# One core, eight sequences: own orders for the first and last turn, the loop written out, the LoRA in two token halves, layernorm a turn earlier

## The chip, the core and the metric

The kernel runs on one core of a Trainium2 chip. The metric is the device time of one launch in microseconds. A launch handles 8 sequences of 512 tokens with 128 features.

## What is computed

Each sequence is layer-normalised; the result goes through a selective state-space block with complex states and through a three-layer MLP with weights of plus or minus one, and both are added to the input:

```python
xn = _layernorm(x, axis=-1)
x = x + _L0_attn_ref(xn, ...) + _L0_ffn_ref(xn, ...)
# attention part: projections z, x, B, C, dt; a causal convolution of 4 taps with silu on x, B, C
lora  = jnp.tanh(x @ theta_w1) @ theta_w2            # 128 -> 48 -> 128
theta = jnp.clip(theta_base + lora, -pi/2, pi/2)
log_z = complex(-(lambda_base + eta * theta**2) * dt, theta * dt)
S_t   = exp(log_z_t) * S_(t-1) + B_t * (x_t * dt_t);  y_t = Re(C_t S_t) + x_t * D
g = y * silu(z);  out = (g * rsqrt(mean(g*g) + eps) * norm_w) @ out_proj_w.T
# MLP: 128 (as x, -x) -> 512 -> 512 -> 128 with relu * 2
```

## The kernel before, in words

**Stages and turns.** One sequence n passes through two stages. Its front makes the convolved projections, the phases and decays, and the MLP; its back, one turn later, makes the attention products G, y, the gated result and the output. Turn n does the front of n and the back of n-1, and at its end the first projections of n+1. So turn 0 has no back, turn 7 is the last with a front and has no next sequence, and turn 8 has only a back. Turns 1 to 6 are a hardware loop (`Fori`) of three passes with two turns each, on all five engines. A second, more general pass over all sequences stands behind an `If` and is not entered for these inputs.

**Order.** Every engine executes a list in an order written by hand (`pipelined` of each block); semaphores with counted steps tie the lists together. An instruction that waits holds up all that stand behind it on its engine.

**TensorE (PE).** `lora1` (L1281) multiplies with 48 columns of `TW1`. Then come, for the back, `g_products` (L1360, tiles of 32 rows), which wait for `add_mlp` of the turn before (`s_mo`), and `g_across` (L1370), which waits for GpSimd's Bre and Bim (`s_bk`). `z_products` (L1312), `lora2` (L1317), `dt_spread` (L1323), the transposes of Bre and Bim (L1381), and y (L1392, L1399, L1408, L1428) follow. Then `mlp0` for tiles 0 and 1 (L1331), `out_products` (L1451), the transposes of the next xn (L1264), `mlp0` for tiles 2 and 3, the sums of squares (L1443), `mlp1` (L1341, L1342) in two pairs of tiles with x projections of the next sequence (L1295) behind each, `mlp_out` (L1350), which waits for the last low half of h1, and the B and C projection (L1305).

**VectorE (DVE).** After `add_mlp` (L746): four convolution taps (L555, L558), `layernorm` of n+1 (L501 to L507), the four masked copies of G (L677), theta (L564), phases (L571 to L590), the states, the gating (L734), cumulated decays (L604, L605), the low halves of h0 (L742), products with the decay in PSUM (`decayed`, L648), `final`, xd = x times dt (L546), the steps of dt, the low halves of h1 (L742), `decayed` of U, which waits for GpSimd's U, and `largest` (L670), directly ahead of `add_mlp`.

**ScalarE (ACT).** silu of x, tanh, silu of B and C, silu of z (L992), theta's input `tin` (L996), copies, xn, sine and cosine (L1007 to L1010), relus and exponentials.

**GpSimd (POOL).** rstd of n+1, then `c_rotated` (six operations on 128x512, from the end of L1010), `rms_of` (L1143, waits for the mean squares), `b_times_rotated` (six, L1162 to L1165, giving Ure and Uim) and `b_and_k` (six, L1190 to L1193, giving Bre and Bim). Each triple is two products and their sum or difference.

**SyncE (SP)** loads x two sequences ahead into two buffers, repeats the rows of B and C through DMAs after `silu_bc`, and stores the output.

## Time and profile before

| | us |
|---|---|
| median of 3 timed runs | 372.28 (367.29 to 373.07) |
| the profiled execution, own time | 364.21 |
| its span, first to last instruction | 361.6 |
| PE busy | 301.3 (83%) |
| DVE busy | 270.0 (75%) |
| POOL busy | 199.6 (55%) |
| ACT busy | 173.9 (48%) |

The span is what the rows below add up to; the execution's own time is 2.6 us more. Shares of busy time are means over the whole span. Matmuls overlap each other, so the time between the starts of two groups says more than the length of one.

### The profile page before, as it was taken

Reading aid. Unit: us, or ns where it says so; the run is one execution under the profiler, and the core shown is the slowest. Engines: PE = TensorE matmul, PEld = TensorE weight load, DVE = VectorE, ACT = ScalarE, POOL = GpSimd, SP = SyncE. Lnnn points to the kernel's source line nnn. Section 1 sums busy time; section 2 is a strip of 40 time slices with the busy share of each in tenths; the row PEclk is TensorE's granted clock in tenths of the full one; section 3 lists DMA queues with packets and bytes.
Section 4 is the critical chain, followed back from the end, with each engine's and each line's share of the span. In section 5 each row is a group of like instructions: output and inputs, shape, how many; then the busy total and the mean of one; then the engine's idle time right before and its main releaser. Section 6 shows DMA issues by size and latency. Waiting matters only on the chain.

```text
span 361.6 us, 9844 instructions
## 1 busy us (share of the span) xinstructions
PE 301.3 (83%) x3887; PEld 211.1 (58%) x3887; DVE 270.0 (75%) x661; ACT 173.9 (48%) x305; POOL 199.6 (55%) x172
## 2 busy tenths in 40 slices
PE   0477079998999898999999997989998999884780
PEld 0353035776577655675667665766676667643670
DVE  2698767698869896798789885789698968973321
ACT  0306752477446834486438732683467446651010
POOL 0000399318881789138952896078926891499201
PEclk9999759999999999999999998999999999998996
DMA  6200400131113110320113011311032101300001
GB/s 179 53 1 4 106 9 0 34 83 38 29 32 77 44 32 8 77 67 2 29 54 96 2 29 33 92 29 29 3 82 66 31 2 46 75 8 24 2 2 34
DMA packets 19095, 14.81 MB, mean 41 GB/s; under 512 B 5045, under 2 KB 14826, under 8 KB 19050
## 3 DMA queue, kind: packets, MB, share of 16 engines
q1 hardware_dynamic: 16090, 13.67, 14.6%
q10 hardware_dynamic: 2960, 0.49, 0.8%
q8 instruction: 34, 0.56, 0.6%
q14 instruction: 11, 0.09, 0.1%
HBM read 3.67 MB, written 2.10 MB: 16 GB/s over the span
## 4 chain that ended last, share of the span: by engine, by line
PE 50%; DVE 34%; issue 6%; ACT 3%; POOL 3%; DMA 2%; SPq 1%; DVEq 0%; POOLq 0%
PE bank L1295 11%; PE bank L1341 7%; PE bank L1342 7%; PE bank L1350 4%; PE bank L1428 3%; PE bank L1443 3%; DVE GT L677 3%; DVE bcsum L558 3%; DVE phl L572 3%; DVE cum L604 3%; PE bank L1360 2%; DVE gT L734 2%; DVE h0l L742 2%; DVE cum L605 2%; PE bank L1293 2%
## 5 line engine op out<-in xcount | busy, mean ns | idle before, releaser
L1341 PE MATMUL bank<-h0h,W 128*128 128x512 f16 x128 | 50.0, 390 | 2.2 <-DVE h0l L742 1.4
L1342 PE MATMUL bank<-h0l,W 128*128 128x512 f16 x128 | 49.8, 389 | 0.0
L1162 POOL TENSOR_TENSOR btmp<-cres,Xre 128x512 f32<-128x512 f32 x8 | 10.2, 1272 | 71.0 <-ACT Xre L1010 71.0
L1295 PE MATMUL bank<-XW,xh 128*128 128x256 f16 x256 | 48.7, 278 | 0.0
L1137 POOL TENSOR_TENSOR rstd<-vare,minus_half 128x4 f32<-128x4 f32 x8 | 8.4, 1049 | 53.2 <-DVE negmean L507 53.2
L1295 PE MATMUL bank<-XW,xl 128*128 128x256 f16 x128 | 35.5, 277 | 0.0
L1042 ACT ACTIVATE h1h<-bank 128x512 f16<-128x512 f32 x32 | 19.0, 593 | 32.2 <-PE bank L1342 31.3
L1295 PEld LDWEIGHTS bank<-XW,xh 128*128 128x128 f16 x256 | 25.4, 99 | 6.8 <-issue 0.2
L742 DVE SCALAR_TENSOR_TENSOR h0l<-bank,h0h 128x512 f16<-128x512 f32 x32 | 22.1, 689 | 8.1 <-ACT h0h L1042 7.8
L742 DVE SCALAR_TENSOR_TENSOR h1l<-bank,h1h 128x512 f16<-128x512 f32 x32 | 22.0, 686 | 7.2 <-ACT h1h L1042 7.0
L677 DVE TENSOR_TENSOR GT<-bank,const 128x512 f32<-128x512 f32 x32 | 19.8, 681 | 8.9 <-PE bank L1370 8.9
L1341 PEld LDWEIGHTS bank<-h0h,W 128*128 128x128 f16 x128 | 13.4, 105 | 17.9 <-issue 2.9
L1042 ACT ACTIVATE h0h<-bank 128x512 f16<-128x512 f32 x32 | 18.1, 591 | 7.1 <-PE bank L1332 7.1
L1143 POOL TENSOR_TENSOR rms<-msq,minus_half 128x4 f32<-128x4 f32 x8 | 8.2, 1019 | 23.3 <-DVE msq L738 23.3
L1342 PEld LDWEIGHTS bank<-h0l,W 128*128 128x128 f16 x128 | 12.8, 100 | 14.1 <-issue 1.4
L1392 PE MATMUL bank<-GT,xd 128*64 128x128 f32 x256 | 20.3, 279 | 0.4 <-issue 0.4
L1350 PE MATMUL bank<-W,h1h 128*128 128x128 f16 x128 | 16.4, 228 | 4.8 <-DVE h1l L742 4.8
L746 DVE SCALAR_TENSOR_TENSOR o<-bank,sffn,xtok 128x512 f32<-128x512 f32 x8 | 6.0, 750 | 18.9 <-PE bank L1350 18.9
L1451 PE MATMUL bank<-OW,gT 128*128 128x128 f32 x128 | 16.4, 281 | 4.5 <-DVE gT L734 4.5
L1451 PEld LDWEIGHTS bank<-OW,gT 128*128 128x128 f32 x128 | 14.9, 191 | 8.2 <-DVE gT L734 8.2
L1399 PE MATMUL bank<-skip_eye,x 128*64 128x128 f32 x256 | 19.5, 273 | 0.0
L558 DVE SCALAR_TENSOR_TENSOR bcsum<-bank,cw,bcsum 128x511 f32<-128x511 f32 (+2 forms) x24 | 18.0, 749 | 0.8
(201 smaller groups left out, 916.7 us busy)
## 6 DMA issues: line engine op xcount, KB each, us to landing
xtok<-in_x SPq DMA_DIRECT2D x8, 256.0 KB, 2.7
cres<-bc SPq DMA_DIRECT2D x32, 64.0 KB, 2.1
cims<-bc SPq DMA_DIRECT2D x32, 64.0 KB, 2.1
bres<-bc SPq DMA_DIRECT2D x32, 64.0 KB, 2.4
bims<-bc SPq DMA_DIRECT2D x32, 64.0 KB, 2.1
out<-osb SPq DMA_DIRECT2D x8, 256.0 KB, 2.3
const<-constants SPq DMA_DIRECT2D x1, 576.0 KB, 5.6
KT<-in_in_proj_w SPq DMA_DIRECT2D x1, 320.0 KB
```

Of the source, the lines that this page charges most:

```text
L558: step(V.scalar_tensor_tensor(bcsum[:, late:], bank[2][:, 0:T - late], cw[:, 2, k:k + 1], bcsum[:, late:], ALU.mult, ALU.add), linked=k > 0)
L572: step(V.tensor_tensor_scan(phl[:], c_("restart"), ph[:], 0.0, ALU.mult, ALU.add), linked=False)
L677: V.tensor_tensor(GT[:, h, :, :], gbanks[fast][h][:].rearrange("p (c t) -> p c t", t=CH), view(const, 0, 128, mask, [[0, NCH], [1, CH]]), ...
L742: V.scalar_tensor_tensor(lo[:, f, :], bank[4 + f % 2][:], 0.0, high[:, f, :], ALU.max, ALU.subtract).then_inc(sig.sem, 1)
L1042: step(sig, A.activation(hi[:, f, :], bank[4 + f % 2][:], ACT.Relu))
L1295: last = M.matmul(dst, tok(x, c, k), w[:, k, :], start=False, stop=(k == TAPS - 1 and q == 2))
L1341: M.matmul(bank[4 + f % 2][:], w, h0h[:, k, :], start=(k == 0), stop=False)
L1342: last = M.matmul(bank[4 + f % 2][:], w, h0l[:, k, :], start=False, stop=(k == MT - 1))
L1350: last = M.matmul(bank[4][:, D * c:D * c + D], h[:, k, CH * c:CH * c + CH], W2[:, k, :], start=(k == 0 and r == 0), stop=(k == MT - 1 and ...
L1392: last = M.matmul(y_part(h, CH * c, CH), xd[:, c, HEAD * h:HEAD * h + HEAD], GT[:, h, c, :], start=(c == 0), stop=True, skip_group_check=True)
L1399: last = M.matmul(y_part(h, CH * c, CH), x2s[p][:, c, HEAD * h:HEAD * h + HEAD], skip_eye[:, h, :], start=False, stop=True, skip_group_che ...
L1451: last = M.matmul(out_in[:, D * c:D * c + D], gT[:, h, CH * c:CH * c + CH], OW[:, h, :], start=(h == 0), stop=(h == 1))
```

## The change

- The loop of turns 1 to 6 is written out on all five engines; the waits have constants in place of registers.
- x has three buffers. SP loads three sequences ahead, and `layernorm(n + 2)` stands right ahead of `add_mlp(n)`; in turn n it no longer stands between taps and G.
- The LoRA works on halves of 256 tokens. `lora1` is six matmuls on two column tiles of 64; tanh works on 128x256; `lora2` is two matmuls on row tiles 0 and 64, the second into bank 1, and stands behind `dt_spread` and behind the wait for two emptied G banks. `tin` is two activations. `theta_w2` is loaded twice, and two memsets fill TW1.
- The gating is four operations of 256 columns in place of two of 512; `out_products` waits for each half of the tokens. The sums of squares stand between `mlp0` tiles 2 and 3, and the first tile of `mlp1` waits for the low halves of h0 one by one.
- The third transposed chunk of Bre, Bim goes to bank 5 and waits for all of G.
- Turn 0 has an order of its own on PE, DVE and ACT, with no other stage between the MLP layers' tiles. In turns 0 and 7 VectorE makes Uim and Bim, in turn 0 also Rim, by three operations each (`other_half`), and GpSimd makes only the real parts. In turn 7 xd stands behind `add_mlp`.

The diff, cut to its core and moved left by 8 columns (in order SP, DVE, ACT, POOL, PE):

```diff
-    (tw2[:], a["theta_w2"]),
+    (tw2[0:LORA, :], a["theta_w2"]),
+    (tw2[HALF:HALF + LORA, :], a["theta_w2"]),
...
+        load(1, 1, 1, None)
+        load(2, 2, 2, None)
         repeat_bc(0, True)
-        with sp.Fori(0, SEQS // 2 - 1) as i:
+        for i in range(SEQS // 2 - 1):
             for p in range(2):
-                load(2 * i + p + 2, 2 * i + p + 2, p)
+                n = 2 * i + p
+                if n + XBUFS < SEQS:
+                    load(n + XBUFS, n + XBUFS, n % XBUFS, n)
                 repeat_bc(2 * i + p + 1, True)
                 store(2 * i + p, 2 * i + p, p)
...
+        step(V.tensor_tensor(shape(tmpa), *first, ALU.mult), linked=False)
+        step(V.tensor_tensor(shape(tmpb), *second, ALU.mult))
+        step(V.tensor_tensor(dst[:], tmpa[:], tmpb[:], op))
+    def whole(t):
+        return t[:]
+    def subs(t):
+        return t[:].rearrange("p (c t) -> p c t", t=SUB)
+    def rotated_im(n):
+        v.wait_ge(c_in.sem, c_in.done(n))
+        v.wait_ge(a_trig.sem, a_trig.done(n))
+        other_half(chain(s_rim, 0), Rim, (cres[:], psn), (cims[:], pcs), ALU.add, whole)
+    def b_times_rotated_im(n):
+        v.wait_ge(b_in.sem, b_in.done(n))
+        v.wait_ge(s_rot.sem, s_rot.done(n))
+        other_half(chain(s_im, EDGES.index(n)), Uim, (bres[:], Rim[:]), (bims[:], Rre[:]), ALU.add, whole)
+    def b_and_k_im(n):
+        step = chain(s_im, EDGES.index(n))
+        step.count[0] = 3
+        br, bi = (view(x, 0, 128, SUB - 1, [[SUB, NSUB], [0, SUB]]) for x in (bres, bims))
+        step.link()
+        v.wait_ge(s_kq.sem, s_kq.at(n, 2))
+        other_half(step, Bim, (subs(Kim), br), (subs(Kre), bi), ALU.subtract, subs)
...
-    def gated(n, p, half):
+    def gated(n, p):
         step = chain(s_gate, n)
-        step.count[0] = half
-        v.wait_ge(t_y.sem, t_y.at(n, half + 1))
-        step(V.tensor_tensor(gT[:, half, :], bank[6 + half][:], z2s[p][:, half, :], ALU.mult), linked=False)
+        v.wait_ge(t_y.sem, t_y.done(n))
+        for lo in (0, T // 2):
+            cols = slice(lo, lo + T // 2)
+            for half in range(2):
+                step(V.tensor_tensor(gT[:, half, cols], bank[6 + half][:, cols], z2s[p][:, half, cols], ALU.mult),
+                     linked=False)
...
         def gates(slot):
             if has_back:
...
                 h0_low(n, 0)
         if has_front:
             bc_taps(n)
-        if next_loaded is not None:
-            layernorm(n + 1, 1 - p, next_loaded)
         if has_back:
             for h in EMPTIED:
                 g_base(n - 1, True, h)
...
             h0_low(n, 2)
+            decayed(n, 0, (0,))
             h0_low(n, 3)
-            decayed(n, 0)
-        if next_loaded is not None:
+            decayed(n, 0, (1,))
+        if has_next:
             xn_low(n + 1)
         if has_back:
             mean_squares(n - 1)
         if has_front:
             decayed(n, 1)
             h1_low(n, 0)
+        if has_front and not has_next:
+            b_times_rotated_im(n)
+            h1_low(n, 1)
+            final(n - 1, pq, stored)
+            h1_low(n, 2)
+            decayed(n, 2)
+            h1_low(n, 3)
+            b_and_k_im(n)
+            largest(n)
+            add_mlp(n, n % XBUFS)
+            x_times_dt(n, p)
+            return
         if has_back:
             final(n - 1, pq, stored)
         if has_front:
             h1_low(n, 1)
-        if next_loaded is not None:
+        if has_next:
             dt_input(n + 1)
         if has_front:
             x_times_dt(n, p)
-        if next_loaded is not None:
+        if has_next:
             dt_steps(n + 1)
         if has_front:
             h1_low(n, 2)
             decayed(n, 2)
             h1_low(n, 3)
             largest(n)
-            add_mlp(n, p)
+            early_layernorm(n + 2)
+            add_mlp(n, n % XBUFS)
+    def first_turn(n, p):
+        bc_taps(n)
+        early_layernorm(n + 1)
+        thetas(n)
+        def lows(slot):
+            if slot < 2:
+                h0_low(n, 2 * slot)
+                h0_low(n, 2 * slot + 1)
+        phases(n, lows)
+        exponents(n, True)
+        rotated_im(n)
+        decayed(n, 0)
+        xn_low(n + 1)
+        decayed(n, 1)
+        h1_low(n, 0)
+        b_times_rotated_im(n)
+        h1_low(n, 1)
+        dt_input(n + 1)
+        x_times_dt(n, p)
+        dt_steps(n + 1)
+        h1_low(n, 2)
+        h1_low(n, 3)
+        decayed(n, 2)
+        b_and_k_im(n)
+        largest(n)
+        early_layernorm(n + 2)
+        add_mlp(n, n % XBUFS)
...
-        pipelined(2 * i + 1, 1, 0, 16 * i + 1, True, True, 16 * i + 32)
-        pipelined(2 * i + 2, 0, 1, 16 * i + 1, True, True, 16 * i + 32)
+    first_turn(0, 0)
+    for i in range(SEQS // 2 - 1):
+        pipelined(2 * i + 1, 1, 0, 16 * i + 1, True, True, True)
...
-        step(a_th, A.activation(tin[:], bank[3][:], ACT.Identity, bias=base[:, 0:1]))
+        for lo, of in ((0, bank[3]), (T // 2, bank[1])):
+            cols = slice(lo, lo + T // 2)
+            step(a_th, A.activation(tin[:, cols], of[:, cols], ACT.Identity, bias=base[:, 0:1]))
...
+            step(a_kt, A.copy(KT[:, 2, :, :], bank[5][:, 0:256]))
         else:
             step(a_kt, A.copy(KT[:, 2:4, :, :], bank[1][:]))
...
+    def first_turn(n, p):
+        silu_x(n, p, 0)
+        silu_x(n, p, 1)
+        tanh_lora(n)
+        dt_repeated(n)
+        silu_bc(n, True)
+        theta_input(n)
+        mlp_high(a_h0, t_h0, h0h, n, (0, 1))
+        silu_z(n, p)
+        mlp_high(a_h0, t_h0, h0h, n, (2, 3))
+        decay_rate(n)
+        normalised(n + 1, (n + 1) % XBUFS)
+        trig(n)
+        decays(n, True, 0)
+        xn_t(n + 1)
+        decays(n, True, 1)
+        mlp_high(a_h1, t_h1, h1h, n, (0, 1))
+        dt_exp(n + 1)
+        mlp_high(a_h1, t_h1, h1h, n, (2, 3))
...
-    def turned(sig, n, re, im, left):
+    def turned(sig, n, re, im, left, other=None):
         (a, b), (c, d) = left
-        for k, (dst, f1, f2, op) in enumerate(((re, c, d, ALU.subtract), (im, d, c, ALU.add))):
+        for k, (dst, f1, f2, op) in enumerate(((re, c, d, ALU.subtract), (im, d, c, ALU.add))[:1 if other else 2]):
             P.tensor_tensor(btmp[0][:], a[:], f1, ALU.mult).then_inc(sig.sem, 1)
             P.tensor_tensor(btmp[1][:], b[:], f2, ALU.mult).then_inc(sig.sem, 1)
             g.wait_ge(sig.sem, sig.at(n, 3 * k + 2))
-            P.tensor_tensor(dst[:], btmp[0][:], btmp[1][:], op).then_inc(sig.sem, 1)
-            g.wait_ge(sig.sem, sig.at(n, 3 * k + 3))
-    def c_rotated(n):
+            if other:
+                g.wait_ge(*other)
...
         if has_next:
             rstds(n + 1)
-        if has_front:
-            c_rotated(n)
+        shared = has_front and not (has_back and has_next)
+        if has_front:
+            c_rotated(n, (s_rim.sem, s_rim.done(0)) if shared and not has_back else None)
         if has_back:
             rms_of(n - 1)
         if has_front:
-            b_times_rotated(n)
-            b_and_k(n, s_kq, 0)
-            b_and_k(n, s_kq, 1)
+            b_times_rotated(n, (s_im.sem, s_im.at(EDGES.index(n), 3)) if shared else None)
+            b_and_k(n, s_kq, 0, (s_im.sem, s_im.done(EDGES.index(n))) if shared else None)
+            if not shared:
+                b_and_k(n, s_kq, 1)
     rstds(0)
     pipelined(0, False, True, True)
-    with g.Fori(0, SEQS // 2 - 1) as i:
+    for i in range(SEQS // 2 - 1):
         pipelined(2 * i + 1, True, True, True)
...
-            last = M.matmul(bank[3][0:LORA, :], w[:], x[:, PAD:], start=(k == 0), stop=(k == 2))
+            for part in range(2):
+                last = M.matmul(bank[3][HALF * part:HALF * part + HALF, 0:T // 2], w[:],
+                                x[:, PAD + T // 2 * part:PAD + T // 2 * part + T // 2],
+                                start=(k == 0), stop=(k == 2), skip_group_check=True)
         last.then_inc(t_l1.sem, 1)
     def x_part(n, half, part):
...
+            rows = slice(HALF * part, HALF * part + LORA)
+            last = M.matmul(into, tw2[rows, :], th1[rows, :], start=True, stop=True)
+        last.then_inc(t_l2.sem, 1)
     def dt_spread(n):
         pe.wait_ge(s_conv.sem, s_conv.done(n))
...
             if f >= 2:
                 pe.wait_ge(s_h1l.sem, s_h1l.at(n, f - 1))
             for k in range(MT):
+                if f == 0:
+                    pe.wait_ge(s_h0l.sem, s_h0l.at(n, max(k, 2) + 1))
                 w = W1[:, k, 128 * f:128 * f + 128]
...
-    def k_transposes(n, chunks):
-        for c in range(chunks):
-            for r, k in enumerate((Bre, Bim)):
-                q = 2 * c + r
-                last = M.transpose(bank[q // 4][:, 128 * (q % 4):128 * (q % 4) + 128], k[:, CH * c:CH * c + CH], ident)
-            if c in (1, chunks - 1):
-                last.then_inc(t_kt.sem, 1)
+    def k_transposes(chunks, into):
+        for q, (c, k) in enumerate((c, k) for c in chunks for k in (Bre, Bim)):
+            last = M.transpose(into[:, 128 * q:128 * q + 128], k[:, CH * c:CH * c + CH], ident)
+        last.then_inc(t_kt.sem, 1)
...
-        pe.wait_ge(s_gate.sem, s_gate.done(n))
         for c in range(NCH):
+            if c % 2 == 0:
+                pe.wait_ge(s_gate.sem, s_gate.at(n, c + 2))
             for h in range(2):
                 last = M.matmul(out_in[:, D * c:D * c + D], gT[:, h, CH * c:CH * c + CH], OW[:, h, :],
...
-            lora2(n)
             dt_spread(n)
         if has_back:
             pe.wait_ge(s_g[True].sem, s_g[True].at(b, 2))
-            k_transposes(b, NST[True])
+        if has_front:
+            lora2(n)
+        if has_back:
+            k_transposes((0, 1), bank[0])
             y_wait(b, True, n if has_front else b)
+            k_transposes((2,), bank[5])
             within(b, 0)
             skipped(1 - p, 0)
             within(b, 1)
...
             last.then_inc(t_y.sem, 2)
+        if has_front and not has_back:
+            mlp0(n, range(MT))
+            mlp1(n, (0, 1))
+            xn_transposed(n + 1)
+            dt_products(n + 1)
+            x_products(n + 1, 1)
+            mlp1(n, (2, 3))
+            x_products(n + 1, 0)
+            mlp_out(n)
+            bc_products(n + 1)
+            return
         if has_front:
             mlp0(n, (0, 1))
         if has_back:
...
         if has_front:
-            mlp0(n, (2, 3))
+            mlp0(n, (2,))
         if has_back:
             sums_of_squares(b)
+        if has_front:
+            mlp0(n, (3,))
         if has_front:
             mlp1(n, (0, 1))
             if has_next:
```

## Rows read from the trace of the kernel before

**Rows 1.** Stretches of the span: length, busy time and count per engine, granted clock, DMA.

```profile
66.05:103.30 37.25, 36.03 (x488) 25.50 (x485) 31.92 (x75) 21.58 (x38) 21.25 (x19) 1.00 0.17 44
140.54:180.12 39.58, 36.32 (x488) 25.68 (x485) 31.94 (x75) 21.47 (x38) 24.90 (x22) 1.00 0.16 42
217.36:258.30 40.94, 37.67 (x489) 26.52 (x485) 31.94 (x75) 21.48 (x38) 24.89 (x22) 0.96 0.16 40
```

**Rows 2.** The chain that ended last, at the loop's first jump back: start, us, what.

```profile
142.97 2.04 issue
```

**Rows 3.** Timeline of PE in turn 2: start, us, line, tiles, count, idle time before.

```profile
105.66 0.40 PE L1281 MATMUL bank<-xh,TW 128*48 128x512 f16 x1
...
106.42 0.50 PE L1360 MATMUL bank<-Ure,Kre 32*128 32x128 f32 x8
106.75 0.40 PE L1360 MATMUL bank<-Uim,Kim 32*128 32x128 f32 x8
...
110.92 1.12 PE L1317 MATMUL bank<-th,tw 48*128 48x512 f32 x2
111.97 0.66 PE L1323 MATMUL bank<-const,dtb 128*128 128x128 f32 x4
...
140.38 0.22 PE L1350 MATMUL bank<-W,h1h 128*128 128x128 f16 x1
```

**Rows 4.** Timeline of DVE in turn 2.

```profile
105.12 0.75 DVE L746 SCALAR_TENSOR_TENSOR o<-bank,sffn,xtok 128x512 f32<-128x512 f32 x1 [2.06 <-PE bank L1350]
...
108.86 0.86 DVE L501 BATCH_NORM_STATS2 st<-xtok 128x6 f32<-128x128 f32 x4
...
110.25 0.16 DVE L507 TENSOR_SCALAR negmean<-mv 128x4 f32<-128x4 f32 x1
...
112.80 0.43 DVE L564 TENSOR_SCALAR theta<-tin 128x512 f32<-128x512 f32 x1
```

**Rows 5.** Timelines of ACT and of POOL in turn 2.

```profile
112.08 0.69 ACT L996 ACTIVATE tin<-bank,base 128x512 f32<-128x512 f32 x1
...
118.82 0.70 ACT L1010 ACTIVATE Xre<-pabs,halfpi 128x512 f32<-128x512 f32 x1
...
128.50 1.02 POOL L1143 TENSOR_TENSOR rms<-msq,minus_half 128x4 f32<-128x4 f32 x1 [1.06 <-DVE msq L738]
...
136.85 1.27 POOL L1165 TENSOR_TENSOR Uim<-btmp 128x512 f32<-128x512 f32 x1
...
143.85 1.27 POOL L1193 TENSOR_TENSOR Bim<-btmp 128x512 f32<-128x512 f32 x1
```

**Rows 6.** Timelines of DVE and POOL where both read SBUF.

```profile
139.96 0.33 DVE L670 TENSOR_TENSOR most<-most,beyond 128x1 f32<-128x1 f32 x1
...
139.21 1.06 POOL L1191 TENSOR_TENSOR btmp<-Kim,bims 128x512 f32<-128x512 f32 x1
...
57.44 1.26 DVE L546 TENSOR_TENSOR xd<-x,dt 128x1024 f32<-128x1024 f32 x1
...
57.70 2.13 POOL L1165 TENSOR_TENSOR Uim<-btmp 128x512 f32<-128x512 f32 x1
```

**Rows 7.** Timelines of PE and DVE in turn 0 and at its end.

```profile
45.65 1.08 PE L1264 MATMUL bank<-const,xn 128*128 128x128 f32 x4 [9.97 <-DVE cum L604]
...
69.18 0.50 PE L1360 MATMUL bank<-Ure,Kre 32*128 32x128 f32 x8
...
67.87 0.75 DVE L746 SCALAR_TENSOR_TENSOR o<-bank,sffn,xtok 128x512 f32<-128x512 f32 x1 [3.40 <-PE bank L1350]
```

**Rows 8.** Timelines of PE and DVE in turns 7 and 8.

```profile
331.78 0.29 PE L1350 MATMUL bank<-W,h1h 128*128 128x128 f16 x1 [4.80 <-DVE h1l L742]
...
335.85 0.50 PE L1360 MATMUL bank<-Ure,Kre 32*128 32x128 f32 x8 [0.84 <-DVE o L746]
...
349.25 2.05 PE L1451 MATMUL bank<-OW,gT 128*128 128x128 f32 x16 [1.41 <-DVE gT L734]
...
329.84 0.69 DVE L648 TENSOR_TENSOR Ure<-Ure,bank 128x512 f32<-128x512 f32 x1 [3.12 <-POOL Uim L1165]
```

More of the change, by code:

```diff
@@ L839, in _ @@
             pair(CB[0:1, :], CB[BLK:BLK + 1, :], cb_row[:], BIAS_SCALE)
-            pair(TW1[0][:], TW1[1][:], tw1[:])
+            for k in range(2):
+                setup(V.memset(TW1[k][:, LORA:], 0.0), False)
+            pair(TW1[0][:, 0:LORA], TW1[1][:, 0:LORA], tw1[:])
             v.wait_ge(set_pe, 1)
@@ L1523, in _ @@
             pipelined(0, 0, False, True, True)
[L1524 removed]
+            for i in range(SEQS // 2 - 1):
                 pipelined(2 * i + 1, 1, True, True, True)
```

114 lines of the change are left out of this document (61 added, 53 removed).

## The prediction

> **What bounds the kernel now.** I cut the span at the start of `mlp_out` in each turn and read busy times per stretch. A turn takes 37.25 us, of which PE is busy 36.03 [rows 1]; four of the six turns that end inside the loop are like that. The turns that cross the loop's jump back take 39.58 and 40.94 us [rows 1]. Next I read the chain of waits: at the first jump it holds PE for 2.04 us with no releaser [rows 2], at the second likewise, and after the second the granted clock of the stretch is 0.96. Last I read the timelines of one normal turn, engine by engine [rows 3 to 5], because a PE with 1.2 us idle looks like the bound and may not be.
>
> It is not alone. A second loop runs through GpSimd and has four pieces. (a) From the start of `g_products` at 106.42 [rows 3] through z, `tin` (ends 112.77), theta at 112.80 and the phases to the end of the cosine at 119.52 is 13.1 us [rows 4, 5]. (b) GpSimd's rotations, rms and U, to the end of Uim at 138.12, are 18.6, with 1.06 of waiting for the mean squares [rows 5]. (c) The two decayed products and the last low half, to `mlp_out` at 140.38 [rows 3], are 2.26; the same three operations with nothing else in the way take 1.94 in turn 7 (329.84 to 331.78) [rows 8], so 0.3 is slack. (d) `mlp_out` to the next `g_products` is the rest of the period, 3.28. The sum is 37.24.
>
> **The loop written out.** The excess over 37.24 is 2.34 and 3.70, together **6.0 us**. Passing from one turn to the next inside a pass has no such row. I take all 6.0. The ends are 4.1 (only the two holds of 2.04, if the slow clock behind them returns from another idle stretch) and 6.5, if constants in place of registers also take something from each turn.
>
> **A normal turn, six times.** *Layernorm*: 1.55 us on DVE (108.86 to 110.41) leaves the place ahead of G [rows 4]. It doesn't shorten the path by that: theta at 112.80 follows directly on `tin`, which ends at 112.77 [rows 4, 5]. So what counts is when `tin` comes. At its new place it falls into the 2.06 us for which DVE waits for `mlp_out` [rows 4], 0.5 of which is left. *LoRA*: `lora1` spans 0.76 to the next group, `lora2` 1.05 [rows 3]. Operations on different row tiles overlap in the trace already: eight matmuls of 128 columns on tiles of 32 rows stand in one row of 0.40 us [rows 3]. Halved, they take about 0.43 and 0.53. `lora1` gives 0.33 to (d). `lora2` ends no earlier, since `dt_spread` (0.49) now goes first: 0.49 + 0.53 is today's 1.05. Two activations in place of one of 0.69 are an estimated 0.8, so `tin` is 0.1 late. Between the last matmul of `lora1` (about 106.33) and `g_products` there is 0.1, which I take as the price of a change of tile shape. The Trainium skill (TensorEngine Tiling (Array Packing), Key Properties) says that changing the tiling mode drains the engine; the change adds two such changes a turn, and by that page the six turns would give 1.2 us less, which the trace neither shows nor excludes. *Gates, sums, mlp0 and mlp1*: the new order fills most of PE's 1.2 us of idle time [rows 1], but only the mean squares, some 0.15 earlier, lie on GpSimd's loop. Where PE gets ahead, it waits at `mlp_out` for the last low half, so (c) is 1.95. *Bim* ends 7.0 us after Uim (143.85 + 1.27 against 138.12) [rows 5]; `g_across`, 2.0 behind the start of `g_products`, would come at 1.95 + 2.95 + 2.0 = 6.9 and waits 0.1.
>
> New turn: (a) 13.2, (b) 18.45, (c) 1.95, (d) 2.95, 0.1 for Bim: 36.65 to 36.7. That is **0.55 a turn, 3.3 us** in six. Upper end: PE alone, 36.03 minus 0.8 of LoRA plus some waits, 36.0 a turn, 7 us. Lower end: the layernorm's small operations are held up by GpSimd, below, nothing or slightly less.
>
> **How DVE and GpSimd share SBUF.** xd, two inputs in SBUF, ran from 57.44 to 58.70; GpSimd's operation that started at 57.70 took 2.13 us, where its kind takes 1.27 [rows 5, 6]: it stood for 0.86. The other way round, `largest` on 128x1 started at 139.96 and ended at 140.29, as GpSimd's ended at 140.27 [rows 6]. So such operations exclude each other. That decides what sharing with DVE is worth. Each triple moved to DVE in turns 0 and 7 takes 3.9 us from GpSimd but puts about 2 us of DVE into which GpSimd cannot work: about 2 gained where GpSimd is the path, not 3.9. The Trainium skill (SBUF — State Buffer, Who interferes with whom) speaks of an exclusive lock on a shared port pair, and says that a Vector operation with at most one SBUF input outside the two-port modes doesn't contend. By that rule the moved layernorm's statistics pass freely and only its small scalar operations can be held.
>
> **Turn 7.** `mlp_out` waits 4.80 us at 331.78 for GpSimd's Uim, DVE having waited 3.12 [rows 8]. New: Uim's three operations on DVE start behind the first low half of h1 and end near 325.5, GpSimd's Ure at 326.9. The second low half and `final` then delay the others; the last low half ends near 329.7. So `mlp_out` starts 2.1 earlier, and about 0.9 more goes behind it: from there to `g_products` at 335.85 are 4.07 us, against 3.28 in a normal turn, though B, C and `lora1` are not among them; with 1.9 us of idling before it in place of 4.8, `mlp_out` should run nearer to its normal pace. **3.0 us** plus 0.15 from (b); ends 1.5 and 4. Bim on DVE starts only then and covers itself with `mlp_out`; xd (1.26) behind `add_mlp` is covered by `g_products`.
>
> **Turn 0.** PE idles 9.97 us before 45.65, in the middle of the first sequence's MLP [rows 7]. In the new order the MLP's first tiles fill that gap, and `mlp_out` comes about 2 earlier, at 63.8. But DVE then still has two products, three operations of Bim, `largest` and a layernorm of 1.55, together about 5.1 behind the last low half at 62.7, ahead of `add_mlp`: 67.8, where it starts at 67.87 today [rows 7]. `g_products`, today at 69.18, follows at 68.55: **0.6 us**. The cosine comes 2.4 later than today, since ACT has four h0 tiles, silu of z and the rate first; Rim on DVE gives that back. Ends: 2 lost, 3 gained. More setup (two memsets, a DMA on the ACT queue, one of 256 KB on SP's) lies beside PE's and DVE's longer chain to the first projections: nothing, at most 1 lost.
>
> **Turn 8.** The first half of the outputs waits for 0.7 of gating in place of 1.2, so `out_products`, held 1.41 at 349.25 [rows 8], starts 0.6 earlier, and the end with it. The third transposes behind all of G cost 0.2. **0.4 us**; ends 0 and 1.
>
> **Sum.** 6.0 + 3.3 + 3.1 + 0.6 + 0.4 = 13.4. The profiled execution took 364.21, so its like would take 350.8. The median of the runs is 372.28, 8.1 above that execution. Taking off 13.4 gives 358.9; since part of the spread between runs may come from the jumps and the slow clock behind them, I take 1.9 more: **357 us**.
>
> **Rivals.** *(1) The moved layernorm holds the turn.* In its new place GpSimd is always busy with B and K, and the scalar operations and the memset may each be held for up to one GpSimd operation of 1.06 to 1.27 [rows 5, 6]. Only 0.5 of the 2.06 is spare, and PE needs `add_mlp` about 0.5 later than it needs `mlp_out`'s end. One hold is free, two cost 0.6 a turn, the whole gain. Then the turns stay at 37.2 and the time is 360. No row has a layernorm beside a busy GpSimd. Chance 0.28. *(2) PE is the bound*, (b) being slack that other orders take up: 36.0 a turn, 7 us in place of 3.3, and the time is 353. For it: PE busy 36.03 of 37.25. Against it: the four pieces close exactly. 0.15. *(3) The jumps' cost stays.* The 2 us come back at another point of the code, and the gain is 7.4: 365. Against it: turn 0 into 1 and the middle of each pass show no stall. 0.05. *(4) Slower.* Straight code has to be fetched throughout, and PE stalls as at the jumps, 2.04 us [rows 2], in every turn: seven stalls and the clock behind some, about 19 us in place of 6. With 7.4 gained elsewhere it ends 6 above today, 378. It decides from one stall a turn on. Against it: the two turns of a pass are straight code and run without one. 0.04. *The change doesn't do what it says*: tiles of the LoRA that do not overlap make `tin` 0.5 late, six times, and the time 360 as in (1). 0.06.
>
> **Chances.** My forecast 0.42, (1) with its twin 0.34, (2) 0.15, (3) 0.05, (4) 0.04. The range 348 to 364.5 takes in the first three with the ends of turns 0 and 7. What a measurement here can tell from no change is 2%, 7.4 us, so faster means below 364.8: 0.88; within 0.08; slower 0.04.
>
> **What would show it.** All turns alike, no "issue" row of 2 us between them; a period near 36.7 with `mlp_out` waiting for a low half that follows Uim at once (if it starts without a wait, PE is the bound); `add_mlp` starting at `mlp_out`'s end (later: rival 1); theta right behind `tin`; GpSimd operations of 2 us beside DVE's triples; turn 7 near 34. Wrong would be a stall in straight code, or a turn 0 longer than today's.

## The result and the profile after

| | before | after |
|---|---|---|
| median of 4 timed runs, us | 369.78 (366.02 to 373.07) | 354.38 (353.19 to 356.84) |
| the profiled execution, own time | 364.21 | 354.44 |
| its span | 361.6 | 352.6 |

The ratio is 0.9654, with a 95% interval of 0.9615 to 0.9694: faster, by 3.5%. Each ratio leaves out slow runs, those over 1.5% above the fastest of their kernel (here those of the kernel before above 372 us), so it says about 13 us, where the medians of all runs differ by 15.4. The forecast was 357, in a range of 348 to 364.5. The two spans differ by 9.0 us, though, where the sum said 13.4.

The windows of the changed kernel, cut at the start of `g_products` (columns: window and length, busy time of PE, PEld, DVE, ACT, POOL with instructions, PEclk, DMA share, GB/s):

```profile
69.75:106.94 37.19, 35.57 (x490) 25.55 (x490) 32.20 (x78) 20.66 (x38) 22.38 (x20) 1.00 0.17 44
218.74:256.01 37.27, 35.64 (x491) 25.54 (x489) 32.06 (x78) 21.33 (x39) 24.89 (x22) 1.00 0.17 44
293.30:327.25 33.95, 27.69 (x415) 19.33 (x413) 29.83 (x55) 16.64 (x30) 17.18 (x15) 1.00 0.16 41
327.25:352.60 25.35, 14.15 (x327) 12.63 (x327) 8.11 (x20) 2.11 (x4) 1.51 (x2) 0.87 0.05 14
```

Against [rows 1]: no turn is longer than the others, so what the jumps cost is gone, but a normal turn (a turn from 1 to 6 that no jump and no slow clock lengthens) is still 37.27 where it was 37.25. Over turns 1 to 6 it is 223.55 us for 229.49, 5.9 gained, all of it by the loop. Turn 7 gained 3.2 (33.95 for 37.18), turn 8 0.4, and turn 0 lost 0.6 (`g_products` at 69.75 for 69.18 in [rows 7]). The sum is 9.0.

Why not the normal turn? GpSimd and VectorE of the changed kernel, from their timelines of one turn (start, length, engine, line, what; in brackets the idle time before it and who ended it):

```profile
238.83 1.27 POOL L1277 TENSOR_TENSOR Rim<-btmp 128x512 f32<-128x512 f32 x1
241.43 1.02 POOL L1253 TENSOR_TENSOR rms<-msq,minus_half 128x4 f32<-128x4 f32 x1 [1.34 <-DVE msq L780]
```

```profile
239.33 0.69 DVE L784 SCALAR_TENSOR_TENSOR h0l<-bank,h0h 128x512 f16<-128x512 f32 x1 [0.47 <-ACT h0h L1132]
239.94 0.68 DVE L657 TENSOR_TENSOR Kim<-Xim,bank 128x512 f32<-128x512 f32 x1
240.53 0.69 DVE L521 SCALAR_TENSOR_TENSOR xl<-bank,xh 128x512 f16<-128x512 f32 x1
241.14 0.15 DVE L780 TENSOR_SCALAR msq<-bank 128x4 f32<-128x4 f32 x1
...
253.14 0.86 DVE L510 BATCH_NORM_STATS2 st<-xtok 128x6 f32<-128x128 f32 x4
...
255.02 0.75 DVE L788 SCALAR_TENSOR_TENSOR o<-bank,sffn,xtok 128x512 f32<-128x512 f32 x1 [0.33 <-PE bank L1473]
```

GpSimd's rms waits 1.34 us for the mean squares, where it waited 1.06 [rows 5]. PE starts the sums of squares 1.2 us earlier behind the cosine's end, but VectorE gets to `msq` only behind the low half of tile 3, Kim and xl, and tile 3 now comes later, since the sums stand ahead of it on PE. The same view shows that rival 1 didn't happen: the layernorm ends before `mlp_out` does. The other loss is ahead of theta: z starts 4.70 us after `g_products` for 4.60, `tin` takes 0.84 in two operations for 0.69, and theta waits for it:

```profile
225.39 0.43 DVE L573 TENSOR_SCALAR theta<-tin 128x512 f32<-128x512 f32 x1 [0.81 <-ACT tin L1086]
```

### The profile page after: what moved, and what is told of

It reads as the page before. It is cut to its first block, busy times and chain, and to the rows that moved or that the text cites. A ratio compares the mean times of both kernels' runs of the same rounds, so it can differ in the third digit from the quotient of the medians.

```text
span 352.6 us, 9459 instructions
## 1 busy us (share of the span) xinstructions
PE 297.9 (84%) x3927; PEld 209.6 (59%) x3927; DVE 282.9 (80%) x694; ACT 172.3 (49%) x313; POOL 181.6 (52%) x157
## 4 chain that ended last, share of the span: by engine, by line
DVE 34%; PE 32%; POOL 16%; ACT 8%; issue 6%; DMA 2%; SPq 1%; POOLq 0%; DVEq 0%
POOL btmp L1272 6%; PE bank L1483 5%; POOL btmp L1273 4%; PE bank L1549 4%; PE bank L1564 3%; PE bank L1473 3%; DVE gT L775 3%; PE bank L1431 3%; DVE phl L581 3%; PE bank L1493 3%; DVE cum L613 2%; POOL Ure L1277 2%; POOL Uim L1277 2%; ACT z L1080 2%; POOL rms L1253 2%
## 5 line engine op out<-in xcount | busy, mean ns | idle before, releaser
L1414 PE MATMUL bank<-XW,xh 128*128 128x256 f16 x256 | 51.6, 289 | 0.0
L1414 PE MATMUL bank<-XW,xl 128*128 128x256 f16 x128 | 36.8, 288 | 0.0
L1414 PEld LDWEIGHTS bank<-XW,xh 128*128 128x128 f16 x256 | 26.3, 103 | 8.0 <-issue 0.9
L1132 ACT ACTIVATE h1h<-bank 128x512 f16<-128x512 f32 x32 | 18.1, 589 | 24.9 <-PE bank L1465 24.9
L1473 PE MATMUL bank<-W,h1h 128*128 128x128 f16 x128 | 15.2, 220 | 3.7 <-DVE h1l L784 3.7
L1564 PEld LDWEIGHTS bank<-const,gsq 128*128 128x128 f32 x128 | 15.5, 192 | 1.0
```

Source lines behind the costliest of these rows:

```text
L1132: step(sig, A.activation(hi[:, f, :], bank[4 + f % 2][:], ACT.Relu))
L1414: last = M.matmul(dst, tok(x, c, k), w[:, k, :], start=False, stop=(k == TAPS - 1 and q == 2))
L1473: last = M.matmul(bank[4][:, D * c:D * c + D], h[:, k, CH * c:CH * c + CH], W2[:, k, :], start=(k == 0 and r == 0), stop=(k == MT - 1 and ...
L1564: last = M.matmul(sums_in[:, c:c + 1], gsq[:, half, CH * c:CH * c + CH], all_ones(1), start=(half == 0), stop=(half == 1))
```

## The experiments

Every ratio is to the kernel before, run on the same chip. Within one kernel the timed runs spread over 0.7 to 7 us, so a period (`g_products` to `g_products`, in the profiled execution) tells more than a median here. A part of the spread has a cause that the profiles showed: **in some turns the granted clock falls for 3 to 4 us.**

### The jumps

```diff
-with pe.Fori(0, SEQS // 2 - 1) as i:
+for i in range(SEQS // 2 - 1):
```

The same on SP, DVE, ACT and POOL of the kernel before.

> The kernel before with nothing changed but the loop over turns 1 to 6, which is written out on every engine. Theory A (the jumps cost what the rows show): the turns that followed a jump lose their excess over 37.25 us, 2.3 and 3.7 us, so the profiled execution comes 6.0 us under the 361.6 us span of the kernel before, at 355.6, with every turn at 37.2, and the changed kernel's six equal turns of 37.27 us say that all else in a normal turn came to nothing. The median of the timed runs then falls by at least 6 us; the median of the kernel before lies 5.6 us over its profiled execution, and if that distance is jumps that cost more in other executions, the timed gain is 10 to 12 us and the spread of the timed runs shrinks to under 3 us. Rival B (the jump only shows a delay that something else would cause in these turns anyway): the turns of 39.6 and 40.9 us stay, and the gain is under 2 us.

Median 361.08 (360.29 to 366.65), ratio 0.9836 [0.9764, 0.9907], the span 357.4. Its turns, and two of the kernel before that [rows 1] doesn't hold:

```profile
106.88:144.19 37.31, 36.03 (x486) 25.48 (x485) 31.97 (x76) 21.61 (x38) 24.92 (x22) 1.00 0.17 44
144.19:182.71 38.52, 36.61 (x485) 25.66 (x485) 31.96 (x76) 21.66 (x38) 24.89 (x22) 1.00 0.17 43
182.71:220.02 37.31, 36.03 (x485) 25.49 (x485) 31.97 (x76) 21.61 (x38) 24.90 (x22) 1.00 0.18 44
```

```profile
106.42:145.78 39.36, 36.10 (x486) 25.51 (x485) 33.91 (x79) 21.58 (x38) 26.29 (x23) 1.00 0.19 49
183.24:223.25 40.01, 36.74 (x486) 25.59 (x485) 34.55 (x81) 21.58 (x38) 26.25 (x23) 0.98 0.18 48
223.25:261.42 38.17, 36.95 (x485) 26.42 (x484) 29.29 (x71) 21.48 (x38) 23.53 (x20) 0.97 0.15 36
```

Theory A holds, rival B falls: a turn that had a jump falls from 39.36 to 37.31. The 6.0 of the forecast are thus made up otherwise: two jumps of 2.1, and some 1.6 of slow clock (0.98 and 0.97, PE 0.7 and 0.9 busier) that the first jump didn't have and that straight code shows as well, below. The two jumps by themselves are worth 4.2. The Trainium skill (Runtime: NRT & Kernel Launch, Instruction fetch mechanics) says that a taken branch whose target isn't in the part of the code that is held must wait until it has been fetched; 2.1 us at each jump fit that, but no row here shows a fetch. One turn of e1 is 1.2 longer at full clock, with 0.37 of it a stall without a releaser; its cause stays open. The expected text was off in two numbers: the span came to 357.4 and not 355.6, since of its turns 1 to 6 that one was longer and turn 0 took 0.4 more, and the median fell by 5.2 and not by 6 or more.

### The mean squares

e2 moves them ahead of the low half of tile 3; e3 undoes PE's side of the edit.

```diff
 decayed(n, 0, (0,))
+mean_squares(n - 1)
 h0_low(n, 3)
 decayed(n, 0, (1,))
 xn_low(n + 1)
-mean_squares(n - 1)
```

> The changed kernel with one move on VectorE: mean_squares of the pair before stands ahead of h0_low of tile 3 instead of behind it, Kim and xl. Theory A (the normal turn gained nothing because the sum over mean squares, queued behind a tile that itself came later, holds GpSimd's rms by 1.34 us): the wait of rms falls to under 0.3 us, the stretch from the cosine's end to Uim's end from 18.93 to about 17.7, and the six periods from 37.27 to 36.0 to 36.4; the time falls by 5.5 to 8 us (six or seven turns of 0.9 to 1.27), to 346 to 349. Rival B (TensorE's order bounds the turn: busy 35.64 of 37.27 with the small waits that remain): periods stay above 37.0 and the time within 1.5 us of the changed kernel. Rival C: h0_low of tile 3 and what stands behind it, now later by the sum, holds TensorE's mlp1 and with it mlp_out: the period lengthens by up to 0.5 us, 3 us in all.

Median 355.67 (354.55 to 356.01), ratio 0.9698 [0.9644, 0.9751]; five of the six periods are 37.54 to 37.57, against 37.27. The wait of rms is gone (it follows Rim at once) and nothing is gained. Rival C in its effect, but by another mechanism. PE of e2, then VectorE ahead of that:

```profile
257.04 0.50 PE L1484 MATMUL bank<-Ure,Kre 32*128 32x128 f32 x8 [0.82 <-DVE o L788]
```

```profile
252.41 0.69 DVE L784 SCALAR_TENSOR_TENSOR h1l<-bank,h1h 128x512 f16<-128x512 f32 x1
253.01 1.08 DVE L708 TENSOR_TENSOR most<-most,beyond 128x1 f32<-128x1 f32 x1
254.02 0.86 DVE L510 BATCH_NORM_STATS2 st<-xtok 128x6 f32<-128x128 f32 x4
...
255.33 0.93 DVE L515 TENSOR_SCALAR vare<-mv 128x4 f32<-128x4 f32 x1
256.18 0.16 DVE L516 TENSOR_SCALAR negmean<-mv 128x4 f32<-128x4 f32 x1
256.25 0.74 DVE L788 SCALAR_TENSOR_TENSOR o<-bank,sffn,xtok 128x512 f32<-128x512 f32 x1
```

Two tiny operations, of 128x1 and 128x4, take 1.08 and 0.93 us, each until GpSimd's operation ends. In the changed kernel they took 0.33 and 0.17. That is rival 1, and it appears here, where GpSimd's row is early. The last of the six turns has no layernorm there, and its period is 36.66.

```diff
-mlp0(n, (2,))
+mlp0(n, (2, 3))
 sums_of_squares(b)
-mlp0(n, (3,))
```

> The changed kernel with TensorE's tile 3 of the first MLP product back ahead of the sums of squares (that one edit undone, VectorE's order as changed). Theory A (the edit turned round what it should do: the squares' sums came earlier by one tile, but the tile that VectorE handles ahead of the mean square came later): tile 3 ends some 1.7 us earlier, the sums some 0.5 later, the mean square comes 0.3 to 0.5 us earlier in the turn, and the period is 36.8 to 37.0: 2 to 3 us less in all. Rival B: the sums set the mean square, which comes 0.3 to 0.5 us later, and the period is 37.6 to 37.8: 2 to 3 us more. Rival C: no change within 0.1 us of a turn.

Median 358.58 (355.38 to 359.25), ratio 0.978 [0.9726, 0.9834]; the periods 37.18. The mean square comes 0.64 earlier in the turn and rms waits 0.78 for 1.34, so the direction is A's, but only 0.09 of it reaches the period: by its size this is rival C. The rest, as in e2, meets another bound. PE no longer waits for the last low half at `mlp_out` (0.36 in the changed kernel), and waits 0.65 inside `mlp0` instead:

```profile
236.26 0.39 PE L1453 MATMUL bank<-xh,W 128*128 128x512 f16 x1 [0.65 <-DVE h0l L784]
```

The timed runs are slower all the same: their mean granted clocks are 0.936 to 0.961, against 0.956 to 0.971 of the changed kernel. In its profile turn 8 takes 26.95 at a clock of 0.81, for 25.35 at 0.87. Whether the order causes that is open.

### The layernorm and the maximum

```diff
 bc_taps(n)
+early_layernorm(n + 1)
...
 largest(n)
-early_layernorm(n + 2)
 add_mlp(n, n % XBUFS)
```

> The changed kernel with the mean squares ahead of h0_low of tile 3, as in e2_msq_first, and the layernorm back where the kernel before has it, behind bc_taps of the next turn. In e2 the wait of GpSimd's rms was gone and a wait of 0.82 us of g_products for add_mlp had come: the running maximum took 1.08 and the layernorm's vare 0.93, where each takes 0.17 alone, beside a GpSimd without a pause, and add_mlp stands behind both. Theory A (the layernorm ahead of add_mlp is what ate the gain): the wait of g_products is gone, the period is 36.6 to 36.9, and the time 2.5 to 4 us under the changed kernel's. Rival B (VectorE's row is late by itself, for xd, h1_low and U's growth, or the layernorm, back ahead of G's masks, now holds theta): the period is 37.1 to 37.6 and nothing is gained.

Median 354.99, ratio 0.9657 [0.9616, 0.9698]; the periods 37.26: rival B, to the hundredth of what it was. The waits of PE in one turn of e6 (wait, us in total, times, longest):

```profile
PE bank L1550 <- DVE S L751: 0.6, 1, 0.6
PE bank L1439 <- DVE GT L715: 0.5, 1, 0.5
PE bank L1381 <- DVE cum L613: 0.4, 1, 0.4
```

Ahead of G's masks the layernorm makes `lora2` wait 0.5 for a bank, a wait that the changed kernel hasn't, and VectorE waits again for `mlp_out` (1.06). So there is a **second row of the same length**, PE and VectorE in turns, and e6 traded one for the other. e8 adds e4's edit and puts the maximum behind `add_mlp`, where it delays the taps.

```diff
-largest(n)
 add_mlp(n, n % XBUFS)
+largest(n)
```

> e6_msq_first_norm_back with two more: turn 0's Bim back on GpSimd as in e4_bim0_gpsimd, and the running maximum behind add_mlp instead of ahead of it. Theory A (the causes add up): turn 1 starts 2 us earlier (67.55 against 69.75 in e4), the period is 36.5 to 36.8 as in e6 or 0.1 less, and the time is 4.5 to 6.5 us under the changed kernel's, 348 to 350. Rival B (TensorE's granted clock falls in some turns, as in three turns of e4, which took 0.8 us more each at a mean of 0.96, whenever it runs with fewer waits): the periods vary, and a part of the gain of up to 3 us is lost again.

Median 354.60, ratio 0.9651 [0.9612, 0.9691]; the periods 37.55, 0.29 more than e6. Theory A misses, and no normal turn shows the slow clock of rival B. The maximum takes 0.40 there beside GpSimd's triple for Bim, ahead of the taps and G's masks, and `lora2` waits 0.83 for the masks where it waited 0.55 in e6: the row that now sets the turn.

e9 gives each its free place: mean squares as in e2, the layernorm ahead of `add_mlp` as in the changed kernel, the maximum in the next turn, where VectorE waits for `tin`. It also has e4's edit of turn 0, below.

```diff
 g_base(n - 1, True, h)
+largest(n - 1)
 thetas(n)
...
-largest(n)
 early_layernorm(n + 2)
 add_mlp(n, n % XBUFS)
```

> e2_msq_first (mean squares ahead of h0_low of tile 3) with the running maximum taken out of VectorE's row ahead of add_mlp and put into the next turn, behind G's masks, where VectorE waits 0.8 us for tin and GpSimd is idle; the layernorm stays ahead of add_mlp; turn 0's Bim is on GpSimd as in e4_bim0_gpsimd. Theory A (two rows of equal length: GpSimd's, which the mean squares shorten to about 36.0, and the one between VectorE and TensorE, which in e6 stands at 37.26 with 0.5 of it a wait for G's masks behind the layernorm): with neither the layernorm ahead of the masks nor the maximum ahead of add_mlp, the period falls to 36.6 to 36.9, 2.5 to 4 us in six turns, and TensorE's waits of 0.6 for S and 0.4 for the running sum stay. Rival B (the layernorm's vare is still held beside GpSimd and add_mlp comes late, as in e2): 37.0 to 37.3, with a wait of g_products of 0.2 to 0.5 us. Rival C (something not seen in the rows keeps 37.2): no change.

Median **350.87** (350.17 to 353.09), ratio 0.958 [0.9501, 0.9659], span 349.4. Its windows (a turn as five of the six are, and the one that isn't), and the waits of PE in the first of them:

```profile
216.63:253.28 36.65, 35.41 (x492) 25.54 (x490) 32.48 (x78) 21.33 (x39) 25.03 (x22) 1.00 0.17 45
141.97:180.00 38.03, 36.90 (x492) 26.13 (x490) 32.37 (x78) 21.44 (x39) 26.34 (x23) 0.96 0.17 43
```

```profile
PE bank L1547 <- DVE S L751: 0.7, 1, 0.7
PE bank L1378 <- DVE cum L614: 0.4, 1, 0.4
```

Theory A: 36.65, the number that the forecast gave the change itself, though by another row. Neither rms nor the growth of U waits for anything here, so GpSimd's loop has slack; PE's 35.4 of work and its waits of 0.7 and 0.4 set the turn. This version has the lowest median of all (its interval overlaps that of the changed kernel; the periods, 36.63 to 36.65 in five turns for 37.19 to 37.29 in six, do not; the two were not timed side by side). The layernorm's vare still takes 0.94, but ends in time. One turn of the six took 38.03 at a mean clock of 0.96; e4 below has three like it. The windows of 2.5 us in one of those show the dip:

```profile
85.05:87.55 2.50, 2.50 (x20) 2.07 (x20) 2.01 (x4) 1.12 (x2) 2.42 (x3) 0.92 0.02 7
87.55:90.05 2.50, 2.50 (x7) 0.88 (x6) 1.90 (x5) 1.64 (x4) 1.26 (x1) 0.50 0.00 0
90.05:92.55 2.50, 2.50 (x18) 1.11 (x16) 1.90 (x5) 1.90 (x5) 2.27 (x3) 0.90 0.00 0
```

PE is busy throughout, at half clock (1.2 GHz) for about 3.4 us of it, and runs 7 matmuls in the middle window.

### The LoRA in halves

e5 puts the form of before into the changed kernel, e12 into e9.

```diff
-    for part in range(2):
-        last = M.matmul(bank[3][HALF * part:HALF * part + HALF, 0:T // 2], w[:],
+    last = M.matmul(bank[3][0:HALF, :], w[:], x[:, PAD:], start=(k == 0), stop=(k == 2))
...
-for lo, of in ((0, bank[3]), (T // 2, bank[1])):
+step(a_th, A.activation(tin[:], bank[3][:], ACT.Identity, bias=base[:, 0:1]))
...
 z_products(n)
+lora2(n)
 dt_spread(n)
```

> The changed kernel with LoRA's two products and the input of theta back in the form of before (three products of 512 columns and one, one operation of ScalarE for tin, ahead of the spread of dt). Theory A (in a normal turn the halves cost what they gave: z starts 4.70 us after g_products against 4.60 before, tin takes 0.84 in two operations against 0.69 in one, and theta now waits for it): theta comes 0.1 to 0.25 us earlier after g_products, the first product costs TensorE 0.3 us more at the turn's end, and the period stays 37.2 to 37.4. Rival B (the halves are worth the 0.3 and more that the forecast gave them, and more than they cost on ScalarE): the period grows by 0.3 us or more, to 37.6, 2 us in all. Rival C (they cost more than they gave): the period falls to 37.0 or less.

Median 353.03 (352.57 to 353.94), ratio 0.961 [0.957, 0.965]; the periods 37.31 to 37.33, 0.05 more. Theory A. But e5's profile is 1.8 shorter than the changed kernel's, and turn 0 accounts for it: turn 1 starts at 67.87 for 69.75, with a mean clock up to there of 0.90 for 0.83. PE in turn 0 of the changed kernel, then of e5:

```profile
34.39 0.66 PE L1445 MATMUL bank<-const,dtb 128*128 128x128 f32 x4 [1.85 <-DVE bcsum L567]
34.98 0.74 PE L1438 MATMUL bank<-th,tw 48*128 48x256 f32 x4
35.64 0.61 PE L1453 MATMUL bank<-xh,W 128*128 128x512 f16 x1
```

```profile
32.94 1.12 PE L1431 MATMUL bank<-th,tw 48*128 48x512 f32 x2
34.29 0.65 PE L1437 MATMUL bank<-const,dtb 128*128 128x128 f32 x4 [0.22 <-DVE bcsum L567]
34.78 0.38 PE L1445 MATMUL bank<-xh,W 128*128 128x512 f16 x1
```

In turn 0 the spread of dt waits for the taps. The old order fills that wait with `lora2`; the new one puts `lora2` behind it, and the MLP starts 0.9 later (the rest of the 1.9 goes with the clock and isn't taken apart). So the halves, with their order, cost about as much in turn 0 as they can give in six turns.

> e9_msq_first_most_next with LoRA in the form of before, as in e5_lora_serial. In e5, where GpSimd's row still set the turn, the serial form changed the period by 0.05 us. Here TensorE and VectorE's row sets it. Theory A (the halves are worth what the forecast put down only where TensorE is on the path: 0.3 for the first product, 0.5 for the second against the 0.15 that tin costs in two operations): the period rises from 36.64 to 36.9 to 37.2, and the time by 1.5 to 3.5 us, to 352.5 to 354.5. Rival B (they are worth nothing in either row): the period stays within 0.1 of 36.64.

Median 351.31 (349.18 to 353.90), ratio 0.9563 [0.9498, 0.9628]. Four periods are 36.77 to 36.79, two 38.16 and 38.17 at a clock of 0.96:

```profile
140.80:177.58 36.78, 36.13 (x485) 25.48 (x484) 32.47 (x78) 21.46 (x38) 25.02 (x22) 1.00 0.17 45
177.58:215.74 38.16, 37.64 (x485) 26.05 (x484) 32.21 (x78) 21.57 (x38) 26.32 (x23) 0.96 0.17 43
```

Between A and B: the halves are worth 0.14 a turn, 0.8 us in all, and turn 0 takes it back: from the first x projection to the first `mlp0` are 13.4 in e12 and 14.1 in e9. The medians of e9 and e12 don't differ. PE saves 0.7 of busy time (36.13 against 35.41); most of it turns into waits for S.

### tin ahead of z

e11 makes this edit in the changed kernel, e10 in e9. In both `lora2` also waits for the taps.

```diff
+theta_input(n)
 silu_z(n, p)
-theta_input(n)
...
 z_products(n)
-dt_spread(n)
 pe.wait_ge(s_g[True].sem, s_g[True].at(b, 2))
 lora2(n)
+dt_spread(n)
```

> The changed kernel with that one edit: LoRA's second product ahead of the spread of dt, tin ahead of z on ScalarE. Theory A (a piece that both rows share): theta 0.6 us earlier after g_products, the period 36.6 to 36.75, and the time 3 to 4.5 us less than the changed kernel's: 350 to 351.5. Theory A': half of it, if the mean squares' place ties GpSimd's row to TensorE's as well: all of the row moves by 0.6 all the same, so 36.6 again. Rival B (as in e10): the period stays above 37.0.

> e9_msq_first_most_next with LoRA's second product ahead of the spread of dt on TensorE, and tin ahead of z on ScalarE. Theory A (the piece from g_products to theta belongs to both rows; in the changed kernel theta waits 0.81 us for tin, which starts as LoRA's product ends, at 224.4): theta starts as G's masks end, 0.6 us earlier, and the period falls by 0.5 to 0.65 under that of e9, to 36.1 to 36.4; TensorE's 35.6 of busy time is the floor. Rival B (z and KT, 0.7 us later on ScalarE, hold TensorE's new states or the phases wait for the spread of dt): the period falls by less than 0.2 us.

In both, theory A fell. e11 has a median of 356.68, ratio 0.9736 [0.9669, 0.9804], periods of 37.64 to 37.72; e10 354.87, 0.9683 [0.9617, 0.9748], four periods of 37.78 or 37.79, one of 37.19 and one of 38.46 at a clock of 0.96. PE's waits in a turn of e11:

```profile
PE bank L1504 <- ACT z L1080: 0.9, 1, 0.9
PE bank L1380 <- DVE cum L613: 0.4, 1, 0.4
```

The transposes of Bre and Bim waited 0.9 us for z, now later. I had looked for z's readers, not for what stands behind it on PE. It is rival B's place (ScalarE's z), but at a loss of 0.45 and 1.1 a turn, which neither text had.

### The edge turns

In e7 turn 7 runs in the normal order and GpSimd does all of U and B.

```diff
-if has_front and not has_next:
-    b_times_rotated_im(n); ...; b_and_k_im(n); ...
-    return
...
-shared = has_front and not (has_back and has_next)
+shared = has_front and not has_back
```

> The changed kernel with turn 7 in the order of the normal turns and the imaginary halves of U and B there back on GpSimd; turn 0 keeps its own order. Theory A (the forecast's term of 3.1 and the 3.3 seen are this edit): turn 7, from g_products of turn 7 to that of turn 8, goes from 33.9 back to 37.0 to 37.3, and the time rises by 3.0 to 3.5 us. Rival B (a part of it comes from what else is new in turn 7, as h0_low of tile 3 and the halves of the gates): the turn is 35 to 36.5 and the time rises by 1 to 2.5 us.

Median 361.36 (360.79 to 362.14), ratio 0.9835 [0.9793, 0.9877]. Turn 7:

```profile
294.44:331.81 37.37, 28.95 (x414) 20.84 (x412) 26.98 (x49) 16.64 (x30) 24.82 (x21) 0.95 0.15 37
```

That is 3.4 more than 33.95, theory A. The median rose by 7.0, though. In the profile the rest is clock: three of its normal turns took 38.0 to 38.1 at 0.96, and turn 8 took 27.19 at 0.79, for 25.35 at 0.87; turn 0, whose code is the changed kernel's, was 1.1 shorter. In e4 GpSimd makes turn 0's Bim by itself (first line: VectorE's order of turn 0):

```diff
-b_and_k_im(n)
...
-if not shared:
+if not (shared and has_back):
     b_and_k(n, s_kq, 1)
```

> The changed kernel with turn 0's Bim (three operations of VectorE, 2.0 us together, ahead of the layernorm and of add_mlp) back on GpSimd; U's and turn 7's shares stay on VectorE. Theory A (VectorE's tail set the start of turn 1: layernorm ended at 69.0, add_mlp started at 68.96, while mlp_out had ended near 67.75): add_mlp of turn 0 starts about 1.2 us earlier, g_products at 68.5 to 68.7 instead of 69.75, and the time falls by about 1.1 us. Rival B: GpSimd's Bim of turn 0, done by itself later, comes after g_products and holds g_across by a microsecond or more: the time stays or grows by up to 1.5 us.

Median 355.09 (352.98 to 355.40), ratio 0.9665 [0.9602, 0.9727]. `g_products` of turn 1 starts at 67.55, 2.2 earlier than in the changed kernel. VectorE of the changed kernel and of e4 ahead of `add_mlp`:

```profile
65.37 0.69 DVE L660 TENSOR_TENSOR tmpa<-Kim,bres 128x512 f32<-128x512 f32 x1
...
66.69 0.69 DVE L662 TENSOR_TENSOR Bim<-tmpa,tmpb 128x512 f32<-128x512 f32 x1
67.42 0.16 DVE L708 TENSOR_TENSOR most<-most,beyond 128x1 f32<-128x1 f32 x1
67.50 0.86 DVE L510 BATCH_NORM_STATS2 st<-xtok 128x6 f32<-128x128 f32 x4
...
68.96 0.74 DVE L788 SCALAR_TENSOR_TENSOR o<-bank,sffn,xtok 128x512 f32<-128x512 f32 x1
```

```profile
64.19 0.68 DVE L658 TENSOR_TENSOR Uim<-Uim,bank 128x512 f32<-128x512 f32 x1
64.79 0.55 DVE L708 TENSOR_TENSOR most<-most,beyond 128x1 f32<-128x1 f32 x1
65.27 0.86 DVE L511 BATCH_NORM_STATS2 st<-xtok 128x6 f32<-128x128 f32 x4
...
66.73 0.74 DVE L788 SCALAR_TENSOR_TENSOR o<-bank,sffn,xtok 128x512 f32<-128x512 f32 x1
```

Theory A in its mechanism, but not in its size. The start of turn 1 moves by itself as well. With the changed kernel's turn 0 it stands at 69.75, 69.26 (e2), 69.20 (e3) and 68.61 (e7), at mean clocks up to there of 0.83, 0.85, 0.90 and 0.90. Against e2, at the same clock and with `mlp_out` starting at the same time, e4 gains 1.7. But e9, which has e4's edit and no maximum there, starts turn 1 at 68.69, behind a setup 0.6 later than e7's: its `add_mlp` waits 1.06 for `mlp_out`, so PE takes over before all of the 1.7 is gained. In the changed kernel's own profile `mlp_out` starts 1.4 later than in e2, at 66.00, and no more than about 1.0 was to be had (an estimate from the 2.0 between `mlp_out` and an `add_mlp` that waits for it in e9). The gain doesn't show in the time, because three normal turns of e4 took 38.05 to 38.14 at 0.96.

## Why the prediction held, and where it didn't

The time fell into the range and near the forecast, but partly by luck, as the last point says. The loop and turn 7 came as described; the normal turn, 3.3 of the 13.4, did not.

- **The loop, 6.0.** Measured 5.9 in the profile of the change, and 4.4 over turns 1 to 6 with the loop alone (225.08, with one turn longer by 1.2). I put slow-clock turns down to the jumps; the changed kernel's execution happened to have none. Right in sum, which is luck, not in its parts: 4.2 belong to the jumps.
- **The normal turn, 3.3.** Measured nothing. This is the step that failed, in piece (b): "only the mean squares, some 0.15 earlier, lie on GpSimd's loop". They came 0.3 later behind the cosine's end, at 9.0 us for 8.7, and (b) took 18.93 for the 18.45 of the forecast. I had followed the sums of squares on PE, and not the low half queued ahead of `msq` on VectorE, though I named that order in the kernel. (a) was 13.38 for 13.2: theta waits for `tin` where VectorE had covered it. (c), 1.97, and (d), 2.99, came as said. What was gained in (c) and (d), 0.6, (a) and (b) took back.
- **One loop or two.** "The four pieces close exactly" was taken as proof that GpSimd's loop was the bound. It closed, but so did PE and VectorE's: e2 and e6 free the first by about 1.3 us and stay at 37.3 to 37.6. Only e9, which shortens both, comes to 36.65, and that this is the forecast's number is chance: the forecast's sum was GpSimd's loop, and e9 is held by PE's. Rival 2 priced PE at 36.0; its row stands at 36.65 with 0.7 of waiting for S and 0.4 for the running sum.
- **Rival 1**, held scalar operations: not in the changed kernel, but in e2, with 0.9 and 0.8 us. Both conditions were named, a busy GpSimd and more than one hold, but only one of the two held operations is the layernorm's; the other is the maximum, which I hadn't counted.
- **The LoRA, 0.33 and more a turn**: it overlaps as said (`lora1` 0.45 and `lora2` 0.63 in the trace), but is worth 0.05 a turn in the changed kernel and 0.14 in e9, and its new order costs turn 0 some 0.7 to 0.9, which I had put at nothing.
- **Turn 7, 3.1**: 3.2 in the trace, 3.4 by e7. `mlp_out` waited 1.52 for 4.80 [rows 8], where I had said 1.9. In the turn it started 2.0 earlier, and 1.3 more was gained behind it, for 2.1 and 0.9.
- **Turn 8, 0.4**: 0.4 in the two profiles, but e1, which has the old gating, takes 25.39 as well, against 25.35. From the start of turn 8 to the last output operation (`osb`) it is 18.50, for 18.70 before and 18.71 in e1. So the new order is worth 0.2; the rest lies in the tail behind it, which varies by 0.4 between profiles of the same code, and is luck.
- **Turn 0, 0.6 gained**: 0.6 lost in the two profiles, inside its ends of 2 lost and 3 gained. That isn't shown to be the change: the same turn 0 ended 1.1 earlier in e7, and at like clocks the new one is level or ahead (68.61 and 69.20 for 69.18 at 0.90; 69.26 for the 69.57 of e1 at 0.85). The row of VectorE behind the last low half was no longer than I said, 4.7 for 5.1; it began late, at 64.26 for 62.7. The cosine came 3.6 later than before, where I had said 2.4: the forecast left out `lora2` behind the spread of dt, which waits for the taps there. With the old order of the two, in e5, the cosine comes 1.1 to 1.7 earlier than in the four profiles of the new turn 0, and turn 1 starts at 67.87, at a clock of 0.90.
- **The time.** The forecast's fall, 372.28 to 357, was 15.3, and the medians fell by 15.4. That is luck. The sum was 4.4 too high in the profile, and a fourth run of the kernel before, of 366.02, took its median from 372.28 to 369.78. The ratio says about 13. The rest is the base: the profiled execution of before was 1.8 to 5.6 us under the medians of the same kernel in five comparisons (366.03 to 369.78), and the changed kernel's was at its own median.

## What to carry to other kernels

Before a wait is priced, the instructions queued ahead of the one that ends it must be followed, each with what releases it; the wait's end is theirs, not the producer's. When one loop's pieces close on the period, look for a second loop that closes too, by the waits that remain on the busiest engine; a gain needs both shortened, and an experiment that frees one and changes nothing has found the other. Turns whose granted clock differs are set aside before a cost is read off their length.
